# PixArt chain of four layers, seen from one core: item 0's first scores ahead of item 1's maxima, later contexts, weights and queries sent behind item 1's keys

## The chip, the cores and the metric

One core of a Trainium2 chip runs the whole program in one launch. The metric is device time in microseconds (us) of that launch; lower is better. The engines that matter are TensorE (PE, with its weight loads PEld), VectorE (DVE), ScalarE (ACT), GpSimd (POOL) and the queue that issues the transfers (SyncE, SP).

## The reference

Eight batch items with 56 query tokens of 128 features pass four layers in turn. Each attends to a context of 1500 tokens of the same item. Layer 0, which the change is about, is a cross attention with 16 heads of 8 features:

```python
xq = _ada_ln(x_q, t_vec, Wss_q, bss_q)
xkv = _ada_ln(x_kv, t_vec, Wss_kv, bss_kv)
q = (xq @ Wq + bq).reshape(B, Lq, nh, dh)
kv = (xkv @ Wkv + bkv).reshape(B, Lkv, 2, nh, dh)
...
```

Softmax of the scaled scores over the 1500 keys, the weighted sum of the values and a projection follow, added to x. Layer 1 is a small mixture of experts with one attention to the context; layers 2 and 3 are transformer blocks with self attention over the 56 tokens, cross attention to the same context, and an MLP. All of it is float32.

## The kernel before

**Two long attentions.** Class `Attention` makes the cross attention of layer 0 (`a0`, eight items, one per batch) and those of layers 2 and 3 together (`a1`, sixteen items). Around them stand shorter stages (`Dense`, `Evidence`, `Own`, `Half`).

**Split products.** To get float32 scores from bf16 products, queries and keys are each split into three bf16 parts. Six pairs of parts (`SLOTS`) are stacked on the partition axis, seven rows per head, in `kstack` (two key stacks, one per parity of the item) and `qstack` (two halves of four batches). `stack_keys` (line 376) sends one DMA per slot and third of the columns, so 18 DMAs per item; `stack_queries` (line 364) sends one per slot and half of the batches, so 12 for all. Both run on SP's queue. Every stack must be cleared first (line 2002 on POOL), and rows 0 and 1 of a key stack are set to ones (line 2149 and following, ACT).

**Steps of an item.** For item i the engines make, by thirds j of the 1500 columns:

- POOL: `deps`, `dpow`, `norm` (the context's norm from its statistics), `hat0` to `hat2` (normalized chunks, line 773), and per third the key's remainder (`rest`, line 782), its second part (`k1.`, line 785) and its third part (`k2.`, line 787). For item 0, `hat1` and `hat2` are made by DVE (line 2259), and POOL only puts a one-element memset there (line 771).
- PE: `T0` to `T2` (transposes, line 559), `K0` to `K2` (key products, 566), `V0` to `V2` (value products, 573), 24 maxima products `M0.0` to `M2.7` (589), `MTa` and `MTb` (579: they turn the maxima into rows), `S0` to `S11` (scores by chunks of 125 keys, 603), `PV0` to `PV5` (614), `OT` and `OTT`.
- ACT: evictions of `T`, `k` and `K` (line 668: first key part, whole key), `V` (674), `shift1` (688), and the exponentials `E0` to `E11` (686).
- DVE: 24 reductions of maxima (line 707), then `maxall`, `maxb`, `part0`, `part1`, `shift0` (710 to 723), and the item's end.
- SP: `load` (the context of a later item) and `s0.j`, `s1.j`, `s2.j` (the three key parts' DMAs, line 380).

The maxima of an item are needed before its scores: `shift0` and `shift1` write them into `qstack`.

**Order of the work.** Each engine's order is written out by hand, by periods. Period p of PE holds the scores of item p, the maxima of item p + 1 and transposes, keys and values of item p + 2; `lead` (line 461) says how far ahead a step is. `template` gives the order, and `EARLY_L0` moves the context's steps for periods -1, 0 and 1 ("T0:M1.2" puts T0 behind M1.2). In period 0 the template begins with M0.0 of item 1, and only then come S0 and S1 of item 0. PE takes its instructions in order, so what stands behind a wait waits too. The products' results go through a ring of three PSUM banks.

**Around the change.** SP (line 1948) first sends x, contexts 0 and 1 into `nat_sb`, then contexts 2 to 4 into free room for statistics alone; then the queries of parts 0 and 1, key part 0 of item 0's first third, the queries of part 2, and the other keys of item 0 (period -2). Then it sends contexts 5 and 6, the modulation weights of the later layers, context 7 and item 2's context, and then the keys of item 1 (period -1). On DVE, `statistics(n)` makes mean and variance of a context by 24 small instructions (lines 2220 and 2222); those of contexts 1 to `STATS_FIRST` - 1 run in a row at the start, the rest in the periods from 0 on, one instruction behind each maximum (`later_statistics`). DVE makes the three query parts by `split` (1711 to 1714), ACT copies them into blocks (`to_blocks`, 1722), and SP sends them.

Of the kernel before, what the change touches and what calls it, by code (L numbers as in the profile page):

```python
# [6 lines left out]
F32 = mybir.dt.float32  # L7
# [24 lines left out]
SHIFT_ROW = 0  # L32
# [20 lines left out]
W_AT, _w = {}, 0  # L53
# [87 lines left out]
HB = B // 2  # L141
# [77 lines left out]
def pixart_program(nc, ctx_nat, ctx_T, x_T, cond_T, weights, vectors, identity, out):  # L219
    ctx = ExitStack()  # L220
    with ctx:
# [6 lines left out]
        def sem(name):  # L228
            return ctx.enter_context(nc.semaphore(name))
# [134 lines left out]
        def stack_queries(sp, ready, stacked, parts=range(3)):  # L364

            for part in parts:
                ready(sp, part)
                for slot, (_, qpart) in enumerate(SLOTS):
                    if qpart == part:
                        rows = slot_rows(slot)  # L370
                        for h in range(2):
                            sp.dma_start(half_queries(rows.start, rows.stop, h, rows.step),
                                         qpart_sb[:, part, HB * h:HB * (h + 1), :, :].rearrange("r b e q -> r (b e q)"))\
                                .then_inc(stacked, 16)
# [23 lines left out]
        class Attention:  # L398
# [73 lines left out]
            def period(self, eng, p, early):  # L472
# [3 lines left out]
                if eng in early.get(p, {}):  # L476
                    context = "TKV" if eng == "pe" else "TkKV"
                    after = dict(x.split(":") for x in early[p][eng].split())
                    fixed = [n for n in order if n[0] not in context]
                    order = [y for x in ["-", *fixed] for y in ([x] if x != "-" else []) + [z for z in after if after[z] == x]]  # L480

# [1134 lines left out]
        class Dense:  # L1616
# [121 lines left out]
            def gated(self, dve, y, gate, t):  # L1738
# [162 lines left out]
        def every_query(d):  # L1901
            return [(d.qstacked, 2 * REPLICA), (d.rows_clear, 1)]
# [13 lines left out]
        for att in (a0, a1):  # L1916
            att.queries_in[0] = every_query(att)
# [3 lines left out]
        keys_cleared = sem("key_stacks_prepared")  # L1921
        keys_restored = sem("key_stack_restored")
# [4 lines left out]
        STATS_FIRST = 5  # L1927
# [20 lines left out]
        def _(sp):  # L1948
# [7 lines left out]
            for n in range(2, STATS_FIRST):  # L1956
                load_context(sp, stats_buffer(n), n, stats_loaded[n])
            stack_queries(sp, queries_ready(d0), a0.qstacked, (0, 1))
            sp.wait_ge(keys_cleared, 1)
            a0.run("sp", sp, -2, beside=lambda name, p: name == "s0.0" and  # L1960
                   stack_queries(sp, queries_ready(d0), a0.qstacked, (2,)))
            for n in range(STATS_FIRST, 7):
                load_context(sp, stats_buffer(n), n, stats_loaded[n])
            w0, w1 = W_AT["L2_W_mod"][0], W_AT["L1_Wq"][0]
            sp.dma_start(w_sb[:, w0:w1], weights[:, w0:w1]).then_inc(loaded_wm, 16)
            sp.wait_ge(stats_done, STATS_AT[2] + 1)
            load_context(sp, stats_buffer(7), 7, stats_loaded[7])
            sp.wait_ge(keys_cleared, 2)
            for p in a0.periods(-1):
                a0.run("sp", sp, p)  # L1970
# [19 lines left out]
        def _(pool):  # L1990
# [10 lines left out]
            for u in range(2):  # L2001
                pool.memset(kstack[:, u, :, :].bitcast(F32), 0.0).then_inc(buffers_ready, 1)  # L2002
            pool.wait_ge(buffers_ready, 2)
# [3 lines left out]
            for p in a0.periods(-2):  # L2007
                a0.run("pool", pool, p)
# [126 lines left out]
        def _(act):  # L2135
# [18 lines left out]
            for u in range(2):  # L2154
                act.wait_ge(buffers_ready, u + 1)
                fill(key_stack(u)[SHIFT_ROW:SHIFT_ROW + 2, :], bf16_ones[:, :], 1.0).then_inc(keys_cleared, 1)
# [10 lines left out]
            a0.run("act", act, -2, only=lambda name: name[0] == "V")  # L2167
            for p in a0.periods(-1):
                a0.run("act", act, p)
# [208 lines left out]
```

## Time and profile before

| what | us |
|---|---|
| three timed runs | 883.29, 888.12, 888.56 (median 888.12) |
| the profiled execution's own time | 883.98 |
| its span in the profile | 882.2 |
| PE busy in the span | 795.9 (90%) |
| DVE, ACT, POOL busy | 593.2, 503.2, 393.2 |

A row of the timeline gives the start in us from the span's start, the length, engine, line, operation, what is written and read, the number of instructions merged, and in brackets the idle time of the engine before it with what ended it. "SPq" is SP's queue at issuing; "PEclk" is TensorE's granted clock as a share of its full speed. "DMA share" is the mean busy share of the 16 DMA engines.

### The profile page before, as it was taken

To read this page: it belongs to the slowest core of one execution; us is meant where nothing else is said; L and a number is where in the kernel's file an instruction comes from. 1 tells how busy PE (TensorE), PEld (TensorE's weight loads), DVE (VectorE), ACT (ScalarE), POOL (GpSimd) and SP (SyncE) were. 2 spreads that over 40 slices of the span, in tenths; PEclk is the share of its full clock that TensorE was granted. 3 is DMA by queue.
4 is the path that set the end of the run, shared out by engine and by line. 5 is a ranking of instruction groups with operands and counts; after the bars stand their busy time and mean duration, and the time that the engine had idled before them with its cause. 6 is when DMAs were issued, how large, how long until landed. Compare 5 with 4: busy or idle time off the path is not lost.

```text
span 882.2 us, 23060 instructions
## 1 busy us (share of the span) xinstructions
PE 795.9 (90%) x9613; PEld 534.1 (61%) x9613; DVE 593.2 (67%) x1301; ACT 503.2 (57%) x786; POOL 393.2 (45%) x519
## 2 busy tenths in 40 slices
PE   6659999999989988687599999999999899999996
PEld 4336667777656634365167777767766676666763
DVE  7947877777623266454667777876778768777834
ACT  8337777776612220343077776666667656666663
POOL 7764766663000500752856666752335505333000
PEclk9689999999999999898689999999999999999999
DMA  8795545436935200440924454433452443543200
GB/s 213 195 232 124 139 112 141 133 91 199 316 118 161 65 20 1 142 108 15 223 63 130 126 141 125 122 89 108 135 162 83 130 131 89 156 130 97 57 3 10
DMA packets 82171, 106.71 MB, mean 121 GB/s; under 512 B 11502, under 2 KB 75758, under 8 KB 81812
## 3 DMA queue, kind: packets, MB, share of 16 engines
q1 hardware_dynamic: 81492, 104.62, 43.2%
q8 instruction: 76, 1.25, 0.6%
q10 hardware_dynamic: 576, 0.63, 0.3%
q14 instruction: 27, 0.22, 0.1%
HBM read 41.37 MB, written 0.23 MB: 47 GB/s over the span
## 4 chain that ended last, share of the span: by engine, by line
PE 72%; DVE 14%; POOL 6%; ACT 4%; issue 2%; DMA 2%; SPq 0%; DVEq 0%; POOLq 0%; ACTq 0%
PE ring_ps L589 14%; PE oacc_ps L614 14%; PE score_ps L603 12%; PE ring_ps L573 7%; PE ring_ps L566 6%; DVE max_sb L707 4%; PE ring_ps L559 3%; PE ring_ps L1644 2%; DMA kstack<-part_sb 2%; DVE tok L1411 1%; PE score_ps L1491 1%; PE ring_ps L579 1%; POOL hat_sb L773 1%; POOL kstack L2002 1%; ACT prob_sb L686 1%
## 5 line engine op out<-in xcount | busy, mean ns | idle before, releaser
L707 DVE TENSOR_REDUCE max_sb<-ring_ps 128x1 f32<-128x500 f32 x576 | 365.9, 672 | 104.0 <-PE ring_ps L589 101.6
L686 ACT ACTIVATE prob_sb<-score_ps 125x896 f32<-125x896 f32 x288 | 255.3, 921 | 85.3 <-PE score_ps L603 84.7
L589 PE MATMUL ring_ps<-kstack,qstack 128*128 128x500 bf16 x576 | 200.4, 391 | 25.9 <-DMA kstack<-part_sb 11.1
L782 POOL TENSOR_TENSOR key_sb<-key_sb,part_sb 128x500 f32<-128x500 f32 x72 | 82.0, 1140 | 189.5 <-ACT key_sb L668 188.9
L603 PEld LDWEIGHTS score_ps<-qstack,kstack 128*128 128x128 bf16 (+1 forms) x2304 | 139.2, 102 | 42.8 <-issue 11.7
L603 PE MATMUL score_ps<-qstack,kstack 128*128 128x112 bf16 (+1 forms) x2304 | 158.2, 215 | 3.1 <-ACT prob_sb L686 2.3
L614 PE MATMUL oacc_ps<-prob_sb,val_sb 125*32 125x168 f32 (+1 forms) x3456 | 139.5, 294 | 0.9 <-ACT prob_sb L686 0.6
L614 PEld LDWEIGHTS oacc_ps<-prob_sb,val_sb 125*32 125x32 f32 x3456 | 97.5, 109 | 49.0 <-issue 19.6
L589 PEld LDWEIGHTS ring_ps<-kstack,qstack 128*128 128x128 bf16 x576 | 51.1, 99 | 90.3 <-DVE max_sb L707 33.6
L787 POOL TENSOR_TENSOR part_sb<-key_sb,part_sb 128x500 bf16<-128x500 f32 x72 | 82.5, 1146 | 5.6
L773 POOL TENSOR_SCALAR hat_sb<-nat_sb,norm_now 125x128 f32<-125x128 f32 x184 | 81.4, 459 | 1.7
L668 ACT ACTIVATE part_sb<-ring_ps,vec_sb 128x500 bf16<-128x500 f32 x72 | 49.0, 680 | 23.7 <-PE ring_ps L566 23.0
L674 ACT COPY val_sb<-ring_ps 125x384 f32<-125x384 f32 x72 | 34.5, 479 | 48.4 <-PE ring_ps L573 48.4
L573 PE MATMUL ring_ps<-w_sb,ctxT_sb 128*125 128x128 f32 x384 | 53.6, 288 | 5.2 <-ACT key_sb L668 2.4
L573 PEld LDWEIGHTS ring_ps<-w_sb,ctxT_sb 128*125 128x125 f32 x384 | 49.6, 198 | 9.7 <-ACT key_sb L668 3.4
L566 PE MATMUL ring_ps<-ctxT_sb,w_sb 128*128 128x500 f32 x96 | 49.6, 608 | 1.2 <-DVE max_sb L707 0.7
L668 ACT ACTIVATE key_sb<-ring_ps,vec_sb 128x500 f32<-128x500 f32 x72 | 48.8, 678 | 0.0
L1688 POOL TENSOR_TENSOR tok_rstd<-tok_var,minus_half 112x4 f32<-112x4 f32 x4 | 4.1, 1034 | 99.7 <-DVE tok_var L1702 99.6
L785 POOL CAST part_sb<-key_sb 128x500 bf16<-128x500 f32 x72 | 43.4, 603 | 4.5
L688 ACT CAST qstack<-ring_ps 2x448 bf16<-2x448 f32 x24 | 12.5, 521 | 49.9 <-PE ring_ps L579 49.9
L559 PE MATMUL ring_ps<-ident,hat_sb 125*128 125x125 f32 x192 | 31.8, 296 | 7.8 <-POOL hat_sb L773 6.8
L759 POOL TENSOR_TENSOR norm_now<-norm_now,minus_half_keys 125x12 f32<-125x12 f32 x16 | 36.7, 2292 | 1.3
(301 smaller groups left out, 1003.2 us busy)
## 6 DMA issues: line engine op xcount, KB each, us to landing
kstack<-part_sb SPq DMA_DIRECT2D x432, 125.0 KB, 2.4
nat_sb<-ctx_nat SPq DMA_DIRECT2D x20, 672.0 KB
qstack<-qpart_sb SPq DMA_DIRECT2D x60, 112.0 KB, 2.3
nat_sb<-ctx_T SPq DMA_DIRECT2D x8, 750.0 KB, 4.4
w_sb<-ctx_nat SPq DMA_DIRECT2D x5, 672.0 KB
w_sb<-weights SPq DMA_DIRECT2D x1, 3268.5 KB, 13.5
kstack<-ctx_T SPq DMA_DIRECT2D x4, 750.0 KB, 13.7
nat_sb<-ctx_nat SPq DMA_DIRECT2D x20, 78.0 KB
```

Of the source, the lines that this page charges most:

```text
L559: last = pe.transpose(ps[:, c * CK:(c + 1) * CK], hat_sb[:, j * CJ + c, :], ident[0:CK, 0:CK])
L566: last = pe.matmul(ps[:, 0:KB], layer.wkey, self.context_T(i)[:, j * KB:(j + 1) * KB], start=True, stop=True)
L573: last = pe.matmul(ps[0:CK, c * D:(c + 1) * D], self.context_T(i)[:, k0:k0 + CK], layer.wval, start=True, stop=True)
L589: last = pe.matmul(ps[:, 0:KB], queries(p, n, D), kstack[:, u, p, j * KB:(j + 1) * KB], start=True, stop=True)
L603: last = pe.matmul(score_ps[0:window(c), c % 2, p // 4, at:at + 2 * LQ], kstack[:, u, p, c * CK:c * CK + window(c)], queries(p, n), start= ...
L614: return pe.matmul(oacc_ps[tile * GW:(tile + 1) * GW, at:at + nh * LQ], val_sb[0:CK, u, c, g * GW:(g + 1) * GW], prob_sb[0:CK, c % PROBS, ...
L668: return act.activation(dst, src, ACT.Identity, bias=layer.bkey)
L686: return act.activation(dst, score_ps[0:CK, c % 2, :, 0:HALF], ACT.Exp)
L707: return dve.tensor_reduce(max_sb[:, p, j:j + 1], ring_ps[:, self.bank[f"{i}.{name}"], 0:KB], AX.X, ALU.max)
L773: last = pool.tensor_scalar(hat_sb[:, c, :], nat_sb[0:CK, u, c, :], norm_now[:, 1, c:c + 1], norm_now[:, 0, c:c + 1], ALU.add, ALU.mult)
L782: return pool.tensor_tensor(rest, rest, part_sb[:, 0, cols], ALU.subtract)
L787: return pool.tensor_tensor(part_sb[:, 2, cols], rest, part_sb[:, 1, cols], ALU.subtract)
```

## The change

Nothing is computed differently. Five orders are changed:

- **PE, period 0:** S0 and S1 (first two chunks of item 0's scores) go ahead of all else in the period. The line stands in `Attention.period`, so it acts on both attentions. In period -1 the order of layer 0's last steps becomes K1, V0, V1, V2, then the products of the maxima, then K2 (before: K1, K2, MTa, MTb, V0, V1, V2); ACT's order follows.
- **Queries:** `stack_queries` can send one half of the batches. Half 0 goes where all went; the six DMAs of half 1 follow behind item 0's keys, with a semaphore of their own that item 4's first maximum waits for.
- **Contexts and weights on SP:** context 4 moves from the start to behind item 0's keys. Contexts 5 and 6 move to the beginning of periods 0 and 1, context 7 and the modulation weights to that of period 2.
- **Statistics:** `STATS_FIRST` is 4, so DVE makes three contexts (1 to 3) in a row at the start, and those of contexts 4 to 7 in periods 0 to 3 (before: 5 to 7 in periods 0 to 2).
- **Second key stack:** POOL clears it behind its step `hat2` of item 0, not at the start; ACT sets its ones behind item 0's values.

```diff
@@ stack_queries
-        def stack_queries(sp, ready, stacked, parts=range(3)):
+        def stack_queries(sp, ready, stacked, parts=range(3), halves=range(2)):
...
-                        for h in range(2):
+                        for h in halves:
@@ Attention.period
+                if eng == "pe" and p == 0:
+                    order = ["S0", "S1", *[n for n in order if n not in ("S0", "S1")]]
@@ EARLY_L0
-            -1: {"pe": "T0:M1.2 T1:M1.6 T2:M2.0 K0:M2.3 K1:M2.7 K2:M2.7 V0:MTb V1:MTb V2:MTb",
-                "act": "T0:- T1:- T2:- k0.0:- K0:- k0.1:- K1:- k0.2:shift1 K2:shift1 V0:shift1 V1:shift1 V2:shift1"},
+            -1: {"pe": "T0:M1.2 T1:M1.6 T2:M2.0 K0:M2.3 K1:M2.7 V0:M2.7 V1:M2.7 V2:M2.7 K2:MTb",
+                "act": "T0:- T1:- T2:- k0.0:- K0:- k0.1:- K1:- V0:- V1:- V2:- k0.2:shift1 K2:shift1"},
@@ queries waited for, statistics
+        later_queries = sem("second_half_queries_stacked")
+        a0.queries_in |= {0: [(a0.qstacked, REPLICA), (a0.rows_clear, 1)], HB: [(later_queries, REPLICA)]}
...
-        STATS_FIRST = 5
+        STATS_FIRST = 4
@@ sync
-            stack_queries(sp, queries_ready(d0), a0.qstacked, (0, 1))
+            stack_queries(sp, queries_ready(d0), a0.qstacked, (0, 1), (0,))
             sp.wait_ge(keys_cleared, 1)
             a0.run("sp", sp, -2, beside=lambda name, p: name == "s0.0" and
-                   stack_queries(sp, queries_ready(d0), a0.qstacked, (2,)))
-            for n in range(STATS_FIRST, 7):
-                load_context(sp, stats_buffer(n), n, stats_loaded[n])
-            w0, w1 = W_AT["L2_W_mod"][0], W_AT["L1_Wq"][0]
-            sp.dma_start(w_sb[:, w0:w1], weights[:, w0:w1]).then_inc(loaded_wm, 16)
-            sp.wait_ge(stats_done, STATS_AT[2] + 1)
-            load_context(sp, stats_buffer(7), 7, stats_loaded[7])
+                   stack_queries(sp, queries_ready(d0), a0.qstacked, (2,), (0,)))
+            stack_queries(sp, queries_ready(d0), later_queries, halves=(1,))
+            load_context(sp, stats_buffer(4), 4, stats_loaded[4])
             sp.wait_ge(keys_cleared, 2)
-            for p in a0.periods(-1):
+            a0.run("sp", sp, -1)
+            for p in a0.periods():
+                if p in (0, 1):
+                    load_context(sp, stats_buffer(p + 5), p + 5, stats_loaded[p + 5])
+                elif p == 2:
+                    sp.wait_ge(stats_done, STATS_AT[2] + 1)
+                    load_context(sp, stats_buffer(7), 7, stats_loaded[7])
+                    w0, w1 = W_AT["L2_W_mod"][0], W_AT["L1_Wq"][0]
+                    sp.dma_start(w_sb[:, w0:w1], weights[:, w0:w1]).then_inc(loaded_wm, 16)
                 a0.run("sp", sp, p)
@@ gpsimd
-            for u in range(2):
-                pool.memset(kstack[:, u, :, :].bitcast(F32), 0.0).then_inc(buffers_ready, 1)
-            pool.wait_ge(buffers_ready, 2)
+            pool.memset(kstack[:, 0, :, :].bitcast(F32), 0.0).then_inc(buffers_ready, 1)
+            pool.wait_ge(buffers_ready, 1)
...
-            for p in a0.periods(-2):
+            a0.run("pool", pool, -2, beside=lambda name, p: name == "hat2" and
+                   pool.memset(kstack[:, 1, :, :].bitcast(F32), 0.0).then_inc(buffers_ready, 1))
+            for p in a0.periods(-1):
                 a0.run("pool", pool, p)
@@ scalar
-            for u in range(2):
-                act.wait_ge(buffers_ready, u + 1)
-                fill(key_stack(u)[SHIFT_ROW:SHIFT_ROW + 2, :], bf16_ones[:, :], 1.0).then_inc(keys_cleared, 1)
+            act.wait_ge(buffers_ready, 1)
+            fill(key_stack(0)[SHIFT_ROW:SHIFT_ROW + 2, :], bf16_ones[:, :], 1.0).then_inc(keys_cleared, 1)
...
             a0.run("act", act, -2, only=lambda name: name[0] == "V")
+            act.wait_ge(buffers_ready, 2)
+            fill(key_stack(1)[SHIFT_ROW:SHIFT_ROW + 2, :], bf16_ones[:, :], 1.0).then_inc(keys_cleared, 1)
```

## Rows read from the trace of the kernel before

**Rows 1.** Busy time by stretch, PE, PEld, DVE, ACT, POOL, granted clock, DMA share, GB/s
```profile
34.80:51.50 16.70, 14.79 (x42) 4.77 (x42) 15.44 (x36) 3.97 (x6) 8.26 (x16) 0.74 0.89 234
51.50:67.70 16.20, 7.16 (x61) 5.72 (x60) 4.62 (x9) 5.99 (x13) 14.59 (x22) 0.79 1.08 224
```
**Rows 2.** The same view by periods of layer 0: period 0, 2 and 3
```profile
64.46:90.50 26.04, 25.07 (x315) 17.62 (x316) 19.91 (x54) 17.83 (x26) 13.61 (x18) 0.94 0.57 137
...
116.70:141.30 24.60, 24.56 (x325) 17.37 (x325) 20.70 (x59) 18.50 (x28) 16.18 (x25) 1.00 0.43 121
141.30:165.60 24.30, 24.25 (x324) 17.29 (x323) 17.93 (x35) 18.51 (x28) 16.37 (x25) 1.00 0.47 128
```
**Rows 3.** Chain of waits up to 110 us: start, us, what
```profile
32.40 2.40 DMA kstack<-part_sb
...
52.69 11.73 DMA kstack<-part_sb
```
**Rows 4.** Timeline of SP's queue, 7 to 70 us
```profile
21.38 6.46 SPq L372 DMA_DIRECT2D qstack<-qpart_sb  x10
...
40.81 0.59 SPq L361 DMA_DIRECT2D w_sb<-ctx_nat  x1
...
49.01 13.64 SPq L380 DMA_DIRECT2D kstack<-part_sb  x18
```
**Rows 5.** Timeline of the start, all engines
```profile
1.22 10.13 POOL L2002 MEMSET kstack<- 128x6000 f32 x2
...
8.34 10.28 ACT L2149 ACTIVATE kstack<-bf_ones 2x6000 f32<-2x6000 f32 x2
...
10.82 0.59 DVE L2248 TENSOR_SCALAR vec_half<-vec_sb 128x63 f32<-128x63 f32 x1
...
11.44 1.11 POOL L1688 TENSOR_TENSOR tok_rstd<-tok_var,minus_half 112x4 f32<-112x4 f32 x1
...
11.70 0.23 DVE L2250 CAST ident_b<-ident 128x128 bf16<-128x128 f32 x1
...
19.01 0.09 POOL L771 MEMSET hats_seen<- 1x1 f32 x1 [0.80 <-DVE hat_sb L2259]
...
19.57 0.40 DVE L1711 CAST prob_sb<-tok 128x448 bf16<-128x448 f32 x1
...
20.21 1.14 ACT L1722 COPY qpart_sb<-prob_sb 64x448 bf16<-64x448 bf16 x2
...
21.75 2.42 DVE L2220 BATCH_NORM_STATS2 bn_tmp<-nat_sb 125x6 f32<-125x128 f32 x12
...
24.54 1.13 POOL L782 TENSOR_TENSOR key_sb<-key_sb,part_sb 128x500 f32<-128x500 f32 x1 [5.45 <-ACT key_sb L668]
...
35.49 6.53 DVE L707 TENSOR_REDUCE max_sb<-ring_ps 128x1 f32<-128x500 f32 x11
```
**Rows 6.** Timeline of periods -1 and 0, 50 to 100 us
```profile
50.04 1.89 PE L566 MATMUL ring_ps<-ctxT_sb,w_sb 128*128 128x500 f32 x4
...
51.51 1.13 POOL L787 TENSOR_TENSOR part_sb<-key_sb,part_sb 128x500 bf16<-128x500 f32 x1
51.54 1.13 DVE L714 TENSOR_SCALAR maxb<-max 128x8 bf16<-128x8 f32 x1
...
54.95 0.66 ACT L668 ACTIVATE part_sb<-ring_ps,vec_sb 128x500 bf16<-128x500 f32 x1
...
54.97 2.88 PE L573 MATMUL ring_ps<-w_sb,ctxT_sb 128*125 128x128 f32 x24 [0.48 <-DVE qstack L723]
...
62.06 5.16 POOL L773 TENSOR_SCALAR hat_sb<-nat_sb,norm_now 125x128 f32<-125x128 f32 x12
...
72.92 0.59 PE L559 MATMUL ring_ps<-ident,hat_sb 125*128 125x125 f32 x4
...
79.14 1.14 POOL L782 TENSOR_TENSOR key_sb<-key_sb,part_sb 128x500 f32<-128x500 f32 x1 [11.91 <-ACT key_sb L668]
```
**Rows 7.** Timeline of PE where the second attention's period 0 begins
```profile
442.87 0.58 PE L589 MATMUL ring_ps<-kstack,qstack 128*128 128x500 bf16 x1 [0.70 <-ACT qstack L688]
```

More of the change, by code:

```diff
@@ L1915, in pixart_program @@
                        {B: next_queries(halves[0]), B + HB: next_queries(halves[1])}, halves, BANKS)
-        for att in (a0, a1):
-            att.queries_in[0] = every_query(att)
+        a1.queries_in[0] = every_query(a1)
         buffers_ready = sem("buffers_ready")
```

## The prediction

> **What bounds the kernel now.** I read the table of stages first, then the chain of waits, then the timelines of the stretches that stood out. The page gives PE 90% of the span, so the question is where PE is not busy. From 116.7 us on, PE fills its stage (24.56 of 24.60, 24.25 of 24.30) [rows 2]: a period of layer 0's attention, some 24.3 us, is PE work, and what is gained ahead of it stays gained. The start is different. Between 51.5 and 67.7 PE has 7.16 us of work in 16.20 while the DMA engines are full (share 1.08) [rows 1]. The chain of waits gives one piece for it: 11.73 us from 52.69, until item 1's first keys have landed [rows 3]; a key transfer that meets no backlog takes 2.40 [rows 3]. The issue queue shows why: from 40.81 on SP issues nine context and weight transfers, and item 1's eighteen keys follow from 49.01 [rows 4]. They are contexts 5, 6, 7, the 768 KB of modulation weights and item 2's context: 3.9 MB, which at 234 GB/s [rows 1] last 16 us. PE stands at item 1's first maxima, and item 0's scores, which need none of this, are queued behind them.
>
> **The change part by part.** I follow it in order of time; "before" is the profiled execution.
>
> *One clearing of key stacks instead of two ahead of the norm.* POOL clears two stacks from 1.22 to 11.35, 5.07 us each [rows 5]. The value that POOL waits for next was there at 10.8, when DVE went on to the halved vectors [rows 5]. So the chain of norm, normalized chunks and transposes moves up by 0.55 us.
>
> *The second clearing, now behind POOL's step "hat2".* That step is the memset at 19.01 [rows 5], in the new kernel at 18.5, so the clearing runs from 18.6 to 23.7. POOL's next work, the first remainder of the keys, began at 24.54 [rows 5]: the clearing fits POOL's own idle time. But DVE's cast of the queries, at 19.57 before [rows 5], would now fall inside it. What a clearing does to DVE: the halving of 63 columns took 0.59 us from 10.82, until 11.41, and the clearing beside it ended at 11.35 [rows 5]; an 8-column scaling took 1.13 us from 51.54 beside a POOL subtraction from 51.51 of the same 1.13 us [rows 6]. Against it: a 128-column cast took 0.23 us at 11.70, while POOL was in a power of 112x4 (from 11.44, 1.11 us) [rows 5]. The bounds are 0 and the whole clearing; I take the whole, as the nearest row has the same POOL instruction. The cast then ends at 24.0 (23.7 and its own rest) instead of 19.5.
>
> The Trainium skill (SBUF — State Buffer, Who interferes with whom) states that VectorE and GpSimd share a pair of ports as an exclusive lock, that copies, casts and tensor_scalar can take it, and that whoever comes first keeps it for the whole instruction. The trace agrees in the halving's 0.59 us; for this cast beside a clearing no row exists, and by the rule the sum is the forecast's, without it the first rival's.
>
> *What the cast holds up.* Copies of the query blocks wait for it on ACT, and behind them in ACT's order stand item 0's key evictions. From the first block copy (20.21) to POOL's first remainder (24.54) are 4.33 us [rows 5]; from 24.05 on that gives 28.4, 3.85 us later than before. DVE's remaining splitting steps end 1.78 us behind the cast (19.97 to 21.75 before [rows 5]), at 25.78; then come three passes of statistics instead of four. Four passes and the handover lasted from 21.75 to 35.49 [rows 5], 3.43 each, so DVE is free at 36.08, 0.6 us later than before.
>
> *Queries by halves.* SP pays 0.646 us for an issue (6.46 for ten [rows 4]). Before, 18 issues lay between the first block copy and the last key of item 0's first columns; now 12, as six queries wait. From 25.2 (24.05 and the copies' 1.14 [rows 5]) they end at 32.9; with the landing 35.3. That is before DVE's 36.08, so DVE's statistics, not the keys, set the first maximum. The 24 maxima took from 35.49 to about 51.3 [rows 5, 6]; now to 51.9.
>
> *What SP issues next.* The rest of item 0's keys ends at 40.7 (24 issues in all from 25.2), the six later queries at 44.6, context 4 and item 2's context (four issues of some 0.6 [rows 4]) at 47.0. Item 1's first keys become ready at 49.6, 2.6 us later: SP is in time. Ahead of them in the DMA engines are 1.5 MB, 6.6 us at 234 GB/s [rows 1], gone by 51.2. The last of its first keys is ready when the subtraction from 51.51 is done [rows 6], at 53.2 in the new kernel; with issue and landing it is there at 56.3.
>
> *The second stack's ones on ACT.* One fill is 5.14 us (10.28 for two [rows 5]). It follows item 0's values, from about 35 to 40; ACT has 3.97 us of work in the 16.7 us from 34.8 [rows 1], so it costs nothing. Without that cover it would be 5.1 us on item 1's evictions.
>
> *Values ahead of the third key block (period -1).* The three value products are 0.96 us each (2.88 for three [rows 6]). They now lie where PE waited for the maxima's parts, but the third needs the bank that the first one leaves. Key block 1 ended at 50.98 (half of the 1.89 from 50.04 [rows 6]) and now at 51.6; two values follow until 53.5, the third until 54.5, and the products that turn the maxima until 55.1. ACT's shift, behind the third value's eviction, is out at 55.8. Key block 2, another 0.95 us, ends at 56.2, and its first eviction starts at 56.25 instead of 54.95 [rows 6], 1.3 us later. POOL's part of item 1 ends as much later, and the normalized chunks of item 2 begin at 63.35 instead of 62.06 [rows 6].
>
> *First scores ahead of item 1's maxima.* The two chunks of scores run from 56.2 to 57.0, then the maxima begin. Their keys are there at 56.3: the 11.73 us are gone, and period 0 starts at 57.0 instead of 64.4. What is late next: item 2's first transposes. Their place in PE's order is some 8 us into the period, at 65; POOL's first third of the chunks is ready at 63.35 + 1.72 = 65.1. Before, they ran at 72.92 [rows 6]. From there to POOL's remainder at 79.14 [rows 6] and into period 1 everything keeps its distances, as POOL's chain leads. The gain is 72.9 - 65.1 = 7.8 us.
>
> *Statistics.* The same moved order makes DVE do context 4 in period 0 and so on, so that period 3 has a pass that it had not. A period with one took 24.60, one without 24.30 [rows 2]: 0.3 us. The upper bound is period 0's own 26.04 [rows 2], 1.7 us; I take 0.3, as period 0 starts after a wait. Contexts 5 to 7 and the weights now go in periods 0 to 2, at most 2.3 MB in a period, 10 us, needed a period later: nothing.
>
> *The second attention.* The order of period 0 is changed there too. Its first maxima waited 0.70 us for ACT's shift, like the scores [rows 7], so nothing that filled a wait is moved: 0, within 0.6 either way.
>
> **The sum.** 7.8 - 0.3 = 7.5 us of 883.98 (span 882.2 and 1.8 around it): 876.5. The three timed runs are 883.29, 888.12 and 888.56, so the profiled one lies 4.1 below their median; two of these four times are near 883.6 and two near 888.3. A median of the new kernel can fall to either group. I take the middle, 886.0 - 7.5 = 878.5.
>
> **Rivals.**
> *The clearing doesn't hold the cast.* For it: the 0.23 us cast beside POOL's power [rows 5]. Against it: both held rows. The whole start is then 4.5 us earlier, maxima from 31.6, period 0 from 52.5: 12.0 us, 872 by the profile's time, 874 from the middle.
> *Part of the backlog stays.* Six query transfers and 1.5 MB still go ahead of item 1's keys, and SP is only 2.6 us ahead. If the first keys land 4 us after PE wants them, at 61, the gain is 3.5: 880.5, or 882.5 from the middle. Against it: 234 GB/s clears it by 51.2.
> *Slower.* The hold costs what the early clearing saved, and item 1's keys still take 11.73 us to land. They are then there at 53.85 + 11.73 = 65.6, the period starts 1.2 us later than before, and with the 0.3 of the statistics the time is 885.5, or 887.5 from the middle. It decides from the point where these keys land after 64.4. Against it: the transfers ahead of them are 1.5 MB and small queries instead of 3.9.
>
> **Chances.** The forecast 0.68, no hold 0.15, part of the backlog 0.10, slower 0.07. About 1% (8.9 us) is what a measurement of this kernel can tell from no change. The forecast's own spread, 5 to 10 us, passes that line in three cases of ten (0.20), no hold nearly always (0.14): faster 0.34. Slower by over 1% needs the last rival and 7 us more: 0.04. The rest, 0.62, is within 1%. The range goes from no hold on the profile's time (871.5) to the backlog rival with a median in the upper group (888 - 3.5, and a margin: 886).
>
> **What would show it.** Right: DVE's first cast of the queries lasts some 4.9 us and ends with POOL's clearing; the first maximum is reduced near 36; item 1's first maxima run near 57 after two chunks of scores, with no DMA piece of over 4 us in the chain there; item 2's first transposes wait for POOL at 65. Wrong: a cast of 0.4 us (then the maxima start near 31.6), or keys of item 1 landing after 60, or later periods well over 24.6 us.

## The result, and the profile after

| | before | after |
|---|---|---|
| median of the runs on one chip, us | 885.38 (8 runs, 882.73 to 888.56) | 880.62 (8 runs, 877.44 to 881.56) |
| ratio after / before | | 0.9934, 95% interval 0.9910 to 0.9958 |
| the profiled execution, us | 883.98 | 880.5 |
| its span in the profile, us | 882.2 | 878.7 |

The kernel became 4.8 us faster by the medians. The forecast was 878.5, so it is missed by 2.1 us, inside its range.

The stages first: the same view as [rows 1, 2], for the corresponding stretches of the kernel after (first maxima of item 0; the gap behind them; periods 0, 3 and 4).

```profile
34.62:51.50 16.88, 12.55 (x39) 4.75 (x40) 14.70 (x37) 7.93 (x6) 10.84 (x19) 0.80 0.79 216
51.50:57.70 6.20, 5.87 (x52) 4.37 (x51) 4.05 (x7) 4.03 (x10) 5.03 (x6) 1.00 0.70 189
57.70:83.70 26.00, 22.79 (x299) 15.31 (x297) 19.66 (x54) 18.27 (x28) 21.14 (x29) 1.00 0.67 177
134.90:159.40 24.50, 24.46 (x324) 17.26 (x322) 20.74 (x59) 18.52 (x28) 16.44 (x25) 1.00 0.48 127
159.40:183.70 24.30, 24.26 (x324) 17.24 (x323) 17.99 (x35) 18.52 (x28) 16.39 (x25) 1.00 0.45 122
```

The stretch in which PE had 7.16 us of work in 16.20 is now 6.20 long with 5.87 of work, and the DMA engines are at 0.70 there instead of 1.08. But period 0 is no longer full: PE has 22.79 in 26.00, where it had 25.07 in 26.04 [rows 2]. Some of that is less work and not waiting: the 16 products of S0 and S1 now run ahead of this stretch (299 matmuls instead of 315), and the granted clock is 1.00 instead of 0.94. Even so PE is idle for 3.21 us instead of 0.97, and the period is no shorter: part of the wait has moved there. From 134.9 on PE fills its periods as before; the one with a pass of statistics (24.50) is 0.20 longer than the one without.

The timeline of the start, as [rows 5]:

```profile
10.82 0.19 DVE L2258 TENSOR_SCALAR vec_half<-vec_sb 128x63 f32<-128x63 f32 x1
...
18.44 5.10 POOL L2015 MEMSET kstack<- 128x6000 f32 x1
...
19.48 4.30 DVE L1714 CAST prob_sb<-tok 128x448 bf16<-128x448 f32 x1
...
23.82 1.15 ACT L1725 COPY qpart_sb<-prob_sb 64x448 bf16<-64x448 bf16 x2 [3.12 <-DVE prob_sb L1714]
...
28.15 1.14 POOL L785 TENSOR_TENSOR key_sb<-key_sb,part_sb 128x500 f32<-128x500 f32 x1 [4.62 <-ACT key_sb L671]
...
35.76 6.50 DVE L710 TENSOR_REDUCE max_sb<-ring_ps 128x1 f32<-128x500 f32 x11
...
41.71 0.71 PEld L562 LDWEIGHTS ring_ps<-ident,hat_sb 125*128 125x128 f32 x4 [1.05 <-POOL hat_sb L776]
41.72 1.10 PE L562 MATMUL ring_ps<-ident,hat_sb 125*128 125x125 f32 x4 [0.55 <-DVE max_sb L710]
...
43.27 2.44 DVE L710 TENSOR_REDUCE max_sb<-ring_ps 128x1 f32<-128x500 f32 x4 [1.00 <-PE ring_ps L592]
```

DVE's cast of the queries, 0.40 us before, lasts 4.30 and ends 0.24 behind POOL's clearing (18.44 + 5.10 = 23.54). The halving of 63 columns, 0.59 with a clearing beside it, takes 0.19 without. ACT's block copies start behind the cast, and POOL's first remainder at 28.15 instead of 24.54. In the last row DVE waits 1.00 us in the middle of item 0's maxima, behind item 1's first transposes; their weight load waits for POOL's chunk, which is ready at 41.6.

SP's issue queue, as [rows 4]: six later queries, context 4 and item 2's context, the keys of item 1, and then context 5:

```profile
40.56 3.83 SPq L372 DMA_DIRECT2D qstack<-qpart_sb  x6
44.44 0.59 SPq L361 DMA_DIRECT2D w_sb<-ctx_nat  x1
...
50.20 12.05 SPq L380 DMA_DIRECT2D kstack<-part_sb  x18
62.30 1.49 SPq L361 DMA_DIRECT2D w_sb<-ctx_nat  x1
```

Periods -1 and 0, as [rows 6]:

```profile
56.92 0.95 PE L606 MATMUL score_ps<-qstack,kstack 128*128 128x112 bf16 x16
...
57.71 0.58 PE L592 MATMUL ring_ps<-kstack,qstack 128*128 128x500 bf16 x2
...
64.28 5.20 POOL L776 TENSOR_SCALAR hat_sb<-nat_sb,norm_now 125x128 f32<-125x128 f32 x12
...
66.07 0.65 PE L562 MATMUL ring_ps<-ident,hat_sb 125*128 125x125 f32 x4 [0.88 <-POOL hat_sb L776]
...
72.74 1.14 POOL L785 TENSOR_TENSOR key_sb<-key_sb,part_sb 128x500 f32<-128x500 f32 x1 [3.27 <-ACT key_sb L671]
```

Item 1's first maxima follow the two chunks of scores at 57.71 and wait for no transfer. Behind them PE waits 0.94 us for ACT's first exponential (at 59.23) and 0.35 for DVE (at 63.21), and then, at item 2's first transposes, 0.88 us for POOL's normalized chunks. The chain of waits of the kernel after shows the same change of hands. In place of the 11.73 us for keys [rows 3] it has the cast, the maxima and POOL:

```profile
19.48 4.31 DVE prob_sb L1714
...
35.85 5.84 DVE max_sb L710 x10
41.72 1.10 PE ring_ps L562 x4
...
61.73 2.27 POOL norm_now L762
64.28 3.48 POOL hat_sb L776 x8
```

For the experiments I use three more marks that I read from the first and last instructions of the timelines: where layer 0's last exponential ends (247.87 before, 241.81 after: 6.06 us gained), how long the stretch from there to the second attention's first maximum is (178.40 and 179.65), and the rest (455.92 and 457.24). The first mark is the end of this row, before:

```profile
245.28 2.59 ACT L686 ACTIVATE prob_sb<-score_ps 125x896 f32<-125x896 f32 x3 [0.75 <-PE score_ps L603]
```

And after:

```profile
239.22 2.59 ACT L689 ACTIVATE prob_sb<-score_ps 125x896 f32<-125x896 f32 x3 [0.75 <-PE score_ps L606]
```

So the pair of profiles gives back 2.6 us of 6.06 outside layer 0, in code that the change hardly touches.

### The profile page after: what moved, and what is told of

Same layout as the page of the kernel before. It is cut to its first block, busy times and chain, and to the rows that moved or that the text cites. A ratio compares the mean times of both kernels' runs of the same rounds, so it can differ in the third digit from the quotient of the medians.

```text
span 878.7 us, 23060 instructions
## 1 busy us (share of the span) xinstructions
PE 799.3 (91%) x9613; PEld 536.4 (61%) x9613; DVE 596.8 (68%) x1301; ACT 503.3 (57%) x786; POOL 394.0 (45%) x519
## 3 DMA queue, kind: packets, MB, share of 16 engines
q8 instruction: 76, 1.25, 0.6%
## 4 chain that ended last, share of the span: by engine, by line
PE 73%; DVE 17%; ACT 4%; POOL 4%; issue 2%; DVEq 0%; POOLq 0%
PE ring_ps L592 14%; PE oacc_ps L617 14%; PE score_ps L606 12%; PE ring_ps L576 7%; PE ring_ps L569 7%; DVE max_sb L710 4%; PE ring_ps L562 3%; PE ring_ps L1647 2%; DVE tok L1414 1%; PE oacc_ps L353 1%; PE score_ps L1494 1%; PE ring_ps L582 1%; POOL hat_sb L776 1%; DVE bn_tmp L2230 1%; ACT prob_sb L689 1%
## 5 line engine op out<-in xcount | busy, mean ns | idle before, releaser
L353 PE MATMUL oacc_ps<-ident,mean_mat 128*128 128x512 bf16 x140 | 37.8, 407 | 0.0
```

## The experiments

Ratios are to the kernel before on the same chip; its medians there were 885.42 (first four kernels), 884.79 (the next four) and 886.60 (the last two).

**What does the late clearing cost?** The second clearing goes back to the start, all else as after.

```diff
-            pool.memset(kstack[:, 0, :, :].bitcast(F32), 0.0).then_inc(buffers_ready, 1)
-            pool.wait_ge(buffers_ready, 1)
+            for u in range(2):
+                pool.memset(kstack[:, u, :, :].bitcast(F32), 0.0).then_inc(buffers_ready, 1)
+            pool.wait_ge(buffers_ready, 2)
...
-            a0.run("pool", pool, -2, beside=lambda name, p: name == "hat2" and
-                   pool.memset(kstack[:, 1, :, :].bitcast(F32), 0.0).then_inc(buffers_ready, 1))
+            a0.run("pool", pool, -2)
```

> The changed kernel with one part undone: POOL clears the second key stack at the start again, right behind the first. Theory (the clearing behind hat2 holds DVE's cast of the queries, and the whole start with it): the cast falls from 4.30 us to 0.40; the norm chain starts 0.55 later; the first maximum is reduced near 32.0 instead of 35.76, item 0's first scores stand near 53.1 instead of 56.9, and the run takes 3.8 us less than the changed kernel: some 876.8 us where that one takes 880.6. Rival (the start is set by something else, the queries' transfers or DVE's statistics): the cast is short but the first maximum stays within 1 us of 35.8, and the time stays within 1 us of 880.6 or gets 0.5 us longer.

Measured: 874.75 us (4 runs), ratio 0.9889 (0.9862 to 0.9917). The timeline of this kernel:

```profile
19.88 0.39 DVE L1714 CAST prob_sb<-tok 128x448 bf16<-128x448 f32 x1
```

The cast is short again, the first maximum comes at 32.26 (35.76 after), and layer 0 ends at 238.77, 3.0 us earlier than after. The spans of the two profiles differ by more, 872.0 against 878.7; the other 3.6 us lie behind layer 0, of which more below. The medians differ by 5.9, or by 3.3 against the changed kernel's second set of runs (878.02, below). The clearing's new place is a loss.

**Can both be had?** Seven of the eight head pairs are cleared right behind the first stack, in POOL's idle time, and the last pair behind "hat2".

```diff
+            pool.memset(kstack[:, 1, 0:7, :].bitcast(F32), 0.0).then_inc(buffers_ready, 1)
...
-                   pool.memset(kstack[:, 1, :, :].bitcast(F32), 0.0).then_inc(buffers_ready, 1))
+                   pool.memset(kstack[:, 1, 7:PAIRS, :].bitcast(F32), 0.0).then_inc(buffers_ready, 1))
```

> The changed kernel with the second clearing split: seven of eight head pairs are cleared right behind the first stack, in the 4.6 us in which POOL waits for the norm, and the last pair (0.64 us) behind hat2. Theory of the hold: this last clearing ends before the cast begins, the cast takes 0.40 us, and the norm chain keeps its 0.5 us; first maximum near 31.5, time 4.3 us below the changed kernel, some 876.3 us. Rival (the start is set by something else): no change against 880.6.

Measured: 874.64 us (4 runs), ratio 0.9893 (0.9864 to 0.9921). From the timeline of this kernel:

```profile
18.44 0.73 POOL L2016 MEMSET kstack<- 128x750 f32 x1
...
18.98 0.43 DVE L1714 CAST prob_sb<-tok 128x448 bf16<-128x448 f32 x1
...
31.39 6.50 DVE L710 TENSOR_REDUCE max_sb<-ring_ps 128x1 f32<-128x500 f32 x11
...
60.45 5.19 POOL L776 TENSOR_SCALAR hat_sb<-nat_sb,norm_now 125x128 f32<-125x128 f32 x12
...
62.25 0.65 PE L562 MATMUL ring_ps<-ident,hat_sb 125*128 125x125 f32 x4 [0.88 <-POOL hat_sb L776]
```

Layer 0 ends at 238.00: 3.8 us earlier than after and 0.77 earlier than with both clearings at the start. I put that down to the earlier norm, for which 0.55 was expected; it is argued, not shown (see the repeated profiles below). The wait of item 2's transposes for POOL is the same 0.88 us, so everything ahead of it moved together.

**Is it the backlog that held the keys?** The loads of contexts 4 to 7, of the weights and of item 2's context go ahead of item 1's keys again, all else as after.

```diff
-            load_context(sp, stats_buffer(4), 4, stats_loaded[4])
+            for n in range(STATS_FIRST, 7):
+                load_context(sp, stats_buffer(n), n, stats_loaded[n])
+            sp.dma_start(w_sb[:, w0:w1], weights[:, w0:w1]).then_inc(loaded_wm, 16)
+            sp.wait_ge(stats_done, STATS_AT[2] + 1)
+            load_context(sp, stats_buffer(7), 7, stats_loaded[7])
...
```

> The changed kernel with contexts 4 to 7, the modulation weights and item 2's context issued ahead of item 1's keys again; the first scores still stand ahead of the maxima. Theory (the backlog ahead of item 1's keys is what the change removes): 4.6 MB at 234 GB/s last 19.7 us from 44.4, item 1's first keys land near 66, the maxima wait there behind the two early chunks of scores, item 2's transposes run near 74, and the time is some 8 us above the changed kernel, 888, no better than the kernel before. Rival (the early scores give the gain, since ACT and PE then have work while keys land): within 2 us of the changed kernel's 880.6.

Measured: 892.52 us (5 runs), ratio 1.0070 (1.0032 to 1.0108). The chain of waits of this kernel:

```profile
55.00 15.96 DMA kstack<-part_sb
```

PE's timeline, where the first maxima of item 1 now come 13 us behind the chunks of scores:

```profile
58.01 0.95 PE L606 MATMUL score_ps<-qstack,kstack 128*128 128x112 bf16 x16
71.01 1.01 PE L592 MATMUL ring_ps<-kstack,qstack 128*128 128x500 bf16 x2 [12.06 <-DMA kstack<-part_sb]
```

The backlog is the wait, and it is longer than the 11.73 us of before: context 4 now belongs to it as well. The keys came 5 us later than the 66 expected; what held them that much longer is not shown. With this wait the kernel is slower than before.

**Are the loads the whole of it?** The kernel before, with only the new places of the loads and `STATS_FIRST` 4.

```diff
-        STATS_FIRST = 5
+        STATS_FIRST = 4
...
-            for n in range(STATS_FIRST, 7):
-                load_context(sp, stats_buffer(n), n, stats_loaded[n])
...
+            load_context(sp, stats_buffer(4), 4, stats_loaded[4])
...
+                if p in (0, 1):
+                    load_context(sp, stats_buffer(p + 5), p + 5, stats_loaded[p + 5])
```

> The kernel before with only the places of the loads changed: context 4 behind item 0's keys, contexts 5 and 6 at the beginnings of periods 0 and 1, context 7 and the weights at that of period 2, and the statistics one period later each. Queries, clearings, order of the scores, values and third key block stay as before. Theory (the loads are the gain, the moved clearing takes part of it back, the orders on PE are worth little): item 1's keys land near 55.5, its first maximum comes behind item 0's values near 57.6, item 2's transposes near 65.6, and the gain on the kernel before is 7 us, at least the changed kernel's 5.8. Rival (the loads need the scores ahead of the maxima and the values ahead of the third keys): less than 3 us of gain.

Measured: 878.34 us (10 runs), ratio 0.9939 (0.9913 to 0.9964). PE's timeline of this kernel (L589 maxima, L559 transposes):

```profile
59.18 0.37 PE L589 MATMUL ring_ps<-kstack,qstack 128*128 128x500 bf16 x1
...
66.75 0.59 PE L559 MATMUL ring_ps<-ident,hat_sb 125*128 125x125 f32 x4
```

Layer 0 ends at 241.84; after, at 241.81. The loads alone give as much as the whole change, and its other parts about cancel one another. The first maximum is at 35.44 (35.49 before), so the three passes of statistics instead of four are no part of this gain. That the two ends agree to 0.03 us is luck in part. The three value products of item 1, right ahead of the first maximum at 59.18, ran at a lower granted clock (0.67, the third number from the end) than in the profile of before (1.00) and took 1.36 us more. The view by windows for these products alone (PE, PEld, granted clock, DMA share, GB/s), in this kernel:

```profile
55.10:59.34 4.24, 4.24 (x24) 4.05 (x24) 0.67 0.73 203
```

In the kernel before:

```profile
54.97:57.85 2.88, 2.88 (x24) 2.69 (x24) 1.00 1.00 232
```

So the loads alone may be worth some 1 us more than this one profile shows. For the other parts, the next three kernels each have one part undone on top of the split clearing (layer 0's end there: 238.00).

**The new order of values and key block 2 in period -1**, undone: the old `EARLY_L0[-1]`.

```diff
-            -1: {"pe": "T0:M1.2 T1:M1.6 T2:M2.0 K0:M2.3 K1:M2.7 V0:M2.7 V1:M2.7 V2:M2.7 K2:MTb",
+            -1: {"pe": "T0:M1.2 T1:M1.6 T2:M2.0 K0:M2.3 K1:M2.7 K2:M2.7 V0:MTb V1:MTb V2:MTb",
...
```

> The split clearing (874.64 us) with the third key block of item 1 ahead of the maxima's products and the values behind them, as in the kernel before. Theory (the three values fill PE's wait for the maxima's parts, and late keys cost POOL's chain little): the values' 2.9 us go in front of item 0's first scores again, which then start near 55.3 instead of 53.1; POOL has item 2's chunks 1.3 us earlier, but PE reaches the transposes only near 64.2 instead of 62.25; the time is some 2 us longer, 876.6. Rival (POOL's chain is what sets period 0, and the late third block delays it): transposes near 61, time 1.3 us shorter, 873.3.

Measured: 875.60 us (4 runs), ratio 0.9894 (0.9871 to 0.9918). From the timeline of this kernel:

```profile
60.12 5.20 POOL L776 TENSOR_SCALAR hat_sb<-nat_sb,norm_now 125x128 f32<-125x128 f32 x12
...
63.47 0.59 PE L562 MATMUL ring_ps<-ident,hat_sb 125*128 125x125 f32 x4
```

Item 0's first scores start 2.64 us later (55.74 against 53.10), but POOL's chunks come 0.33 earlier, and PE then finds them ready: no wait in brackets. The transposes are 1.22 later, and layer 0 ends at 238.77, 0.77 later. But 0.67 of this is there already at the end of item 0's 24 maxima (49.33 against 48.66), ahead of the edit. That leaves 0.1 for the order, which is nothing that I can tell here; I had expected 2 us.

**The first scores ahead of the maxima**, undone in both attentions.

```diff
-                if eng == "pe" and p == 0:
-                    order = ["S0", "S1", *[n for n in order if n not in ("S0", "S1")]]
```

> The split clearing with item 0's first two chunks of scores behind item 1's first maxima again, in both attentions. Theory (once item 1's keys land in time, nothing waits between the two, and period 0 is set by POOL's chunks of item 2): item 1's first maximum is reduced 0.8 us earlier, item 0's first exponential 0.3 us later, item 2's transposes within 0.5 us of 62.25, time within 1 us of 874.64. First rival (the early scores carry part of the gain): transposes 2 us later, time 2 us longer. Second rival (the early scores cost something in the second attention, where the stretch behind its first maximum is 457.2 to 459.7 us in four kernels that have them and 455.9 and 456.3 in two that have not): that stretch at 456, time 2 us shorter.

Measured: 873.52 us (4 runs, 873.12 to 878.68), ratio 0.9880 (0.9848 to 0.9913). Layer 0 ends at 238.32, 0.32 later; but in this profile the first maximum is already 0.35 late (31.74), ahead of the edit. So this part is worth nothing that I can tell here. The rest behind the second attention's first maximum is 458.45 against 458.79: it costs nothing there either.

**The queries by halves**, undone: all twelve go at the start, on top of the split clearing.

```diff
-            stack_queries(sp, queries_ready(d0), a0.qstacked, (0, 1), (0,))
+            stack_queries(sp, queries_ready(d0), a0.qstacked, (0, 1))
...
-            stack_queries(sp, queries_ready(d0), later_queries, halves=(1,))
```

> The split clearing with the queries of all batches ahead of item 0's keys, 18 issues instead of 12 up to the first columns' last key. Theory (without the hold SP's issues set the first maximum): 6 x 0.646 = 3.9 us more, first maximum reduced near 34.9 instead of 31.39, time 3.5 us longer, some 878.1. Rival (DVE's three passes of statistics set it anyway): first maximum within 0.5 us of 31.4, time within 1 us.

Measured: 877.43 us (4 runs), ratio 0.9912 (0.9888 to 0.9937). The timeline of this kernel:

```profile
20.80 6.45 SPq L372 DMA_DIRECT2D qstack<-qpart_sb  x10
...
34.20 6.07 PE L592 MATMUL ring_ps<-kstack,qstack 128*128 128x500 bf16 x11 [4.60 <-DMA kstack<-part_sb]
...
34.84 5.36 DVE L710 TENSOR_REDUCE max_sb<-ring_ps 128x1 f32<-128x500 f32 x9 [3.36 <-PE ring_ps L592]
```

Ten query issues of 0.645 us stand ahead of the first key, and PE waits for it. The first maximum is 3.45 us later, yet layer 0 ends only 1.98 later (239.98). The 24 maxima tell why: 15.80 us here (34.84 to 50.64), 17.27 with the early start (31.39 to 48.66). Maxima that start early run into item 1's transposes. The first of these waits for POOL in the split kernel:

```profile
37.51 1.10 PE L562 MATMUL ring_ps<-ident,hat_sb 125*128 125x125 f32 x4 [0.71 <-POOL hat_sb L776]
```

DVE then waits 1.16 us for PE, and 0.50 here. That is 0.66 of the 1.47 us. The rest stands at the second and third transposes, which take 1.07 and 1.00 us there at granted clocks of 0.50 and 0.60, and 0.62 each here at 1.00. With the same clock in both, the queries by halves could be worth up to 0.8 us more than 1.98.

From the loads alone (241.84) to the split clearing with everything (238.00) are 3.84 us. One part clearly helps, the queries by halves with 1.98 us; the earlier norm may give up to 0.77, and the two orders on PE nothing that these profiles show. I can't close the sum to better than 1 us: each kernel has one profile, and in that of the loads alone the lower clock stretched the value products by 1.36. The change as it was made loses 3.8 us by the late clearing (238.00 to 241.81), and so arrives where the loads alone do.

**Does POOL's chain decide what is left?** On top of the split clearing, POOL makes the norm of each later item one period earlier, behind the chunks of the item before, so that it no longer stands between the last key part and the next chunks.

```diff
+                if eng == "pool" and self.norms_ahead and p >= -1:
+                    own = ("deps", "dpow", "norm")
+                    rest = [n for n in order if n not in own]
+                    at = rest.index("hat2") + 1
+                    order = [*(own if p == -1 else ()), *rest[:at], *("+" + n for n in own), *rest[at:]]
...
```

> The split clearing with one thing new: in layer 0 POOL makes the norm of a context (2.9 us) one period early, behind the chunks of the item before, where it is idle, from item 2 on. Theory (POOL's chain of item 1's last key part, norm and chunks sets period 0, and that of item 2 the beginning of period 1): item 2's chunks begin 2.9 us earlier, at 57.6, the waits of PE for them (0.88 and 0.47 us in period 0, some 0.7 in period 1) are gone, item 1's first exponential comes 1.5 us earlier than 81.83, and the time is 1.5 to 2.5 us shorter, some 872.6. Rival (PE's and DVE's own work in periods 0 and 1 is as long as POOL's chain): less than 0.5 us.

Measured: 871.87 us (4 runs, 870.59 to 872.78), ratio 0.9847 (0.9826 to 0.9868). The timeline of this kernel:

```profile
57.43 5.20 POOL L786 TENSOR_SCALAR hat_sb<-nat_sb,norm_now 125x128 f32<-125x128 f32 x12
...
61.00 0.59 PE L572 MATMUL ring_ps<-ident,hat_sb 125*128 125x125 f32 x4
...
63.01 2.27 POOL L772 TENSOR_TENSOR norm_now<-norm_now,minus_half_keys 125x12 f32<-125x12 f32 x1
```

The chunks come 3.02 us earlier, the transposes 1.25 and without a wait, and period 1 is shorter by 1.03 (its exponentials start at 80.31, those of period 2 at 105.64; with the split clearing alone 81.83 and 108.19). Layer 0 ends at 235.26, 2.74 earlier; 0.20 of this is there already at the first exponential (54.24 against 54.44). This is the fastest kernel of the study, and its interval lies below that of the change as made.

**How far do two profiles of one kernel agree?** The kernel after and the kernel before, unchanged, once more.

> The changed kernel once more, for a second profile. Theory (the gain is made in layer 0 alone and stays; that the first profiles differ by 3.5 us and the timed medians by some 5 is the stretch between the two long attentions, which varies from run to run with the granted clock): end of layer 0's last exponential again at 241.8 within 0.2 us, the stretch from there to the second attention's first maximum anywhere from 174.9 to 179.7 us, time within 2 us of 880.6. Rival (the changed kernel itself makes the later stretch longer): that stretch again at 179.7 within 0.5 us, longer than the kernel before has it.

> The kernel before once more, for a second profile. Theory (as for the changed kernel): end of layer 0's last exponential again at 247.9 within 0.2 us, so that the gain there is 6.1 us in both pairs of profiles; the stretch from there to the second attention's first maximum differs from 178.4 by up to some 4 us, longer with more time at the lower granted clock. Rival (the later stretch is the same in each run of a kernel): 178.4 within 0.5 us.

Measured: 878.02 us (5 runs), ratio 0.9908 (0.9874 to 0.9942) for the changed kernel; 883.50 (10 runs), ratio 0.9985 (0.9953 to 1.0017) for the one before. Layer 0 of the changed kernel ends at 241.80, to 0.01 us where it ended before. That of the kernel before ends at 248.71, 0.84 later than in its first profile and 0.56 late already at the first maximum: this half of the expectation failed. The second pair of profiles gives a gain of 6.91 us in layer 0, the first 6.06. The start carries the clock as well: item 1's second transposes took 0.62 us in the first profile of the kernel before and 1.07 in its second, at a mean granted clock of 0.53 (44.49 to 45.56). For these transposes alone, first profile:

```profile
43.92:44.54 0.62, 0.62 (x4) 0.39 (x4) 1.00 1.04 278
```

So a difference in layer 0 under some 0.8 us doesn't count here. The order's 0.77 and the norm's 0.77 are of this size, and most of each is there already at the end of item 0's maxima (0.67 and 0.78).

The stretch between the attentions, by windows, in the first profile of the kernel before:

```profile
247.87:426.27 178.40, 146.65 (x1198) 88.50 (x1199) 82.62 (x134) 44.94 (x78) 56.62 (x61) 0.91 0.29 79
```

In its second:

```profile
248.71:423.60 174.89, 143.01 (x1198) 85.41 (x1199) 82.26 (x134) 44.98 (x78) 56.65 (x61) 0.93 0.29 81
```

The kernel after, first profile:

```profile
241.81:421.46 179.65, 148.13 (x1198) 90.02 (x1199) 82.69 (x134) 44.97 (x78) 56.73 (x61) 0.90 0.28 79
```

And second:

```profile
241.80:418.64 176.84, 145.43 (x1198) 87.89 (x1199) 82.59 (x133) 44.99 (x79) 56.60 (x61) 0.91 0.29 80
```

The same 1198 matmuls take 143.0 to 148.1 us of PE, longer where the granted clock (the third number from the end) is lower; DVE, ACT and POOL do not change. The stretch follows PE: 174.89 to 179.65 us. Within one kernel it differs by 3.5 and 2.8 us, between the two by no more than 4.8 with the ranges overlapping: no effect of the change is seen in it.

## Why the prediction was right, point by point

- **Where the wait was.** Right. The 11.73 us for item 1's keys were the backlog ahead of them: the loads alone remove them, and put back they return as 15.96.
- **The clearing holds the cast.** Right; of the two bounds, 0 and the whole clearing, the whole was the one to take. The rule that was weighed (the Trainium skill, SBUF — State Buffer, section Who interferes with whom: whoever comes first keeps the shared ports for its whole instruction) agrees with this case's cast: it ends 0.24 us behind the clearing in three profiles (23.78 behind 23.54 twice, 24.31 behind 24.07), although it started 0.5 us earlier in one of them. Expected were 4.9 us until 24.0. The two kernels without this overlap, or with 0.73 us of clearing, have casts of 0.39 and 0.43: the first rival, "no hold", falls. They also show what it would have been worth: the rival priced the earlier start at 4.5 us on top of the forecast, and without the overlap layer 0 ends 3.0 and 3.8 us earlier (874.75 and 874.64 for its 874 from the middle).
- **What the cast holds up.** First remainder forecast at 28.4, there at 28.15; first maximum 36.08, there at 35.76. The norm chain gained the expected 0.5. Statistics, not keys, set the first maximum, as said; the chain goes from 25.57 through them without a gap.
- **Queries by halves, SP in time, ones on ACT at nothing.** Right. The later queries are issued from 40.56 to 44.4, item 1's first keys from 50.20 (49.6 forecast), and no wait for them is left.
- **The 24 maxima: the mis-sized term.** I let them take 15.8 us as before and end at 51.9. They took 16.73, until 52.49. The step "what the cast holds up" also delays POOL, whose chunks of item 1 come 3.6 us later than before (39.92 against 36.28), while the maxima start only 0.27 later. PE's transposes of item 1 stand between the maxima, and the first of them waits for POOL; DVE then waits 1.00 us for PE, 0.50 before. That is half of the 0.93. The other half is TensorE's clock: the second transposes took 0.62 us before, at a granted clock of 1.00, and 1.06 after:

```profile
44.68:45.74 1.06, 1.06 (x4) 0.68 (x4) 0.56 0.86 207
```

The forecast had no term for the clock, and the maxima of the kernel before took 16.25 us in its second profile. The undone halves show the same two terms from the other side (15.80 against 17.27).
- **What is late next.** The mechanism is right: item 2's transposes wait for POOL. Its time was 65.1 and is 66.07: the 0.6 of the maxima, and 0.3 more up to key block 2's first eviction (57.13 for 56.25). That leaves 6.85 us of the 7.8. "From there everything keeps its distances" was too good: the second group of transposes waits for POOL too (0.47), and the remainder is 6.40 ahead at 72.74.
- **Statistics.** 0.20 us (24.50 against 24.30) for the 0.3 forecast. Gain at the end of layer 0: 6.06 for 7.5 (6.91 in the second pair of profiles).
- **The second attention.** Nothing, as forecast. Its scores now stand first and take the same 0.70 us wait that the maxima had [rows 7], in PE's timeline of the kernel after:

```profile
438.07 1.65 PE L606 MATMUL score_ps<-qstack,kstack 128*128 128x112 bf16 x16 [0.70 <-ACT qstack L691]
```

- **From the profile to the median.** The base, 886.0, came out well, but by luck: it was the middle of two groups of times, and in the eight runs of the result there are no two groups (three of them lie at 885.35 to 885.40). The kernel before had medians of 883.50 to 886.60 here. The forecast's 7.5 us from there make 878.5; layer 0's 6.06 would make 879.9; 880.62 was measured, and 878.02 when the same kernel ran again. The lower end of the range, 871.5, should read 872.0 by its own sum; nothing hangs on it.
- **The rivals.** "Part of the backlog stays" gives a time near the measured one (882.5), but its mark, keys of item 1 that land at 61, is not in the trace: PE took them at 57.71 without a wait. "Slower" did not come; its condition, keys that land after 64.4, is what the loads put ahead bring about (71.0), and the kernel is then 0.7% slower.

## What to carry to other kernels

When one in-order queue feeds a serial start, send what the next stage needs first and let bulk transfers follow it: here that order alone was worth 6 us of layer 0, and the other parts of the change together came out about even. A large memset on GpSimd can hold a VectorE cast until it ends (4.30 us instead of 0.39 here), so put it where VectorE waits for others, in pieces if need be. And once a wait is gone, look at the engine that is late next (here POOL's norm): moving that in turn gave another 2.7 us. And before a small difference is put down to an edit, see whether it is there already ahead of the edit.

## What the runs showed of the hardware that was not expected

- A cast of 128x448 that meets a running clearing lasts 4.30 or 4.80 us instead of 0.39, and then ends 0.24 us behind the clearing, less than its own length alone.
- The stretch between the attentions takes 174.89 to 179.65 us in the four profiles of two kernels, longer at the lower granted clock (0.90 to 0.93 on average), while the full periods from item 4's first exponential to the end of layer 0 take 80.80 and 80.79 us in the two profiles of the kernel after, 80.75 and 80.79 in those of the kernel before. One profile of a kernel that has such a stretch doesn't settle a difference of 3 us in the whole time; the mark at the end of layer 0 does, down to the 0.84 us by which it differed between two profiles of one kernel.
- The same four transposes in the start took 0.62 us at a granted clock of 1.00 and 1.06 or 1.07 at 0.50 to 0.56, in different profiles of unchanged code. Where DVE waits for them, that goes into the time of the maxima.
- With context 4 and the later queries added to the 3.9 MB ahead of them, item 1's keys cost 15.96 us in the chain, more than the 11.73 of the kernel before, though that piece begins only 2.3 us later (55.00 against 52.69).
